# Third attention: two exponentials of each group on VectorE, and the sums two places later in TensorE's program

## What is computed

```python
xh = x.reshape(B, T, H, hd)                      # B=4, T=1024, H=16, hd=8
x_centered = xh - jnp.mean(xh, axis=1, keepdims=True)
corr = jnp.einsum('bthd,bThd->bhtT', x_centered, x_centered)
corr = jax.nn.softmax(corr, axis=-1)
out = jnp.einsum('bhtT,bThd->bthd', corr, xh)
```

## Time and profile before

| what | value |
|---|---|
| median of three runs | 3316.86 us (3312.75 to 3324.0) |
| the profiled execution, its own time | 3323.09 us |
| its span, first to last instruction | 3321.4 us |
| mean granted TensorE clock over the span | 0.941 |
| exponentials of the third attention | 496, first 2779.2 us, last 3242.6 us from the span's start |
| busy share of the span | PE 87%, ACT 72%, DVE 70%, POOL 7% |

### The profile page before, as it was taken

The page is one execution under the profiler, slowest core; times in us unless marked ns, Lnnn a source line. Parts: engine busy times, 40 slices in busy tenths (PEclk is TensorE's granted clock), DMA queues, the critical chain, the costliest instruction groups (busy, mean ns, idle before and its releaser), DMA issues. The chain is left out here.

```text
span 3321.4 us, 53185 instructions
## 1 busy us (share of the span) xinstructions
PE 2874.0 (87%) x17952; PEld 1294.0 (39%) x17952; DVE 2340.6 (70%) x3805; ACT 2377.6 (72%) x3572; POOL 224.3 (7%) x180
## 2 busy tenths in 40 slices
PE   4888888899999578888889999979979756888886
PEld 2221222666776311111147666732237551111115
DVE  6777777677776767777767777779999855443454
ACT  5889889555455679999955555556635657999994
POOL 2000000000000310000010000010000011000002
PEclk8899999999999789999989999989979967999997
DMA  5444552000000544544300000000000004233321
GB/s 130 66 61 59 68 69 42 26 0 1 0 0 1 140 81 59 66 56 65 53 32 0 0 0 0 0 28 1 1 1 0 0 22 104 40 56 47 57 49 28
DMA packets 79832, 125.47 MB, mean 38 GB/s; under 512 B 12984, under 2 KB 32344, under 8 KB 78748
## 3 DMA queue, kind: packets, MB, share of 16 engines
q1 hardware_dynamic: 79612, 122.65, 21.8%
HBM read 87.49 MB, written 29.16 MB: 35 GB/s over the span
## 5 line engine op out<-in xcount | busy, mean ns | idle before, releaser
L1952 ACT ACTIVATE m_mix_hidden<-m_mix_up_ps 128x512 f32<-128x512 f32 x512 | 305.7, 597 | 295.1 <-PE m_mix_up_ps L1868 295.1
L1129 ACT ACTIVATE b_direct_probs<-b_direct_s_ps 128x1024 f32<-128x1024 f32 x512 | 473.6, 1091 | 18.2 <-PE b_direct_o_ps L1036 11.9
L1876 PE MATMUL m_mix_down_ps<-m_w,m_mix_hidden 128*128 128x128 f32 x4096 | 474.8, 276 | 0.0
L1876 PEld LDWEIGHTS m_mix_down_ps<-m_w,m_mix_hidden 128*128 128x128 f32 x4096 | 467.2, 192 | 15.3 <-issue 15.3
L1868 PE MATMUL m_mix_up_ps<-m_mix_ZT,m_w 128*128 128x512 f32 x1024 | 471.8, 619 | 0.0
L1129 ACT ACTIVATE a_direct_probs<-a_direct_s_ps 128x1024 f32<-128x1024 f32 (+10 forms) x512 | 431.8, 938 | 54.7 <-DVE a_direct_s_ps L1167 41.9
L1129 ACT ACTIVATE c_att_probs<-c_att_s_ps 128x1024 f32<-128x1024 f32 x496 | 457.9, 1141 | 6.8 <-PE c_att_s_ps L1012 4.2
L1167 DVE SCALAR_TENSOR_TENSOR a_direct_s_ps<-distance,slopes,a_direct_s_ps 128x512 f32<-128x512 f32 (+3 forms) x512 | 355.3, 732 | 117.7 <-PE a_direct_s_ps L1012 114.7
L1164 DVE TENSOR_TENSOR b_direct_s_ps<-b_direct_s_ps,distance 128x512 f32<-128x512 f32 x512 | 335.8, 695 | 141.9 <-PE b_direct_s_ps L1012 141.0
L1036 PE MATMUL c_att_o_ps<-c_att_probs,c_v_cols 128*32 128x512 f32 x1984 | 274.9, 610 | 50.2 <-ACT c_att_probs L1129 50.2
L1036 PE MATMUL b_direct_o_ps<-b_direct_probs,v_cols 128*32 128x512 f32 x2048 | 275.1, 610 | 14.0 <-DVE b_direct_taken L1153 13.1
(11 more groups left out here) (385 smaller groups left out, 3498.5 us busy)
## 6 DMA issues: line engine op xcount, KB each, us to landing
qk_parts<-b_qkv_parts SPq DMA_DIRECT2D x48, 256.0 KB, 3.5
qk_parts<-a_qkv_parts SPq DMA_DIRECT2D x24, 256.0 KB, 4.9
a_k_rows<-qk_parts SPq DMA_DIRECT2D x32, 192.0 KB
a_q_rows<-qk_parts SPq DMA_DIRECT2D x32, 192.0 KB
b_k_rows<-qk_parts SPq DMA_DIRECT2D x32, 192.0 KB
b_q_rows<-qk_parts SPq DMA_DIRECT2D x32, 192.0 KB
qk_parts<-c_split_parts SPq DMA_DIRECT2D x24, 256.0 KB, 3.0
c_k_rows<-qk_parts SPq DMA_DIRECT2D x32, 192.0 KB
```

Of the source, the lines that this page charges most:

```text
L1129: act.activation(probs[:, J % 2, j, lo:hi], s_ps[:, slot(hg, place), lo:hi], ACT.Exp).then_inc(exped, 1)
L1876: last = pe.matmul(down_ps[:, t % 2, e, :], hidden[:, e * HALVES + h, t * P:(t + 1) * P], w["w2"][:, e * HALVES + h, :], start=(h == 0), s ...
L1952: act.activation(hidden[:, f, :], up_ps[:, f % UP_BANKS, :], ACT.Silu).then_inc(silu_done, 1)
```

## The change

Two units of each group are given instead of one: 31 at place 2 and 30 at place 6, so a group's order is 0, 1, 31, 2, 3, 4, 30, 5, ..., 29. The argument `given` becomes a list for each group, and the counts that the semaphores are compared with follow (`KEPT`, `GIVEN`, `NG`); `power` has a buffer for each given unit. VectorE's program reads the second given unit right after the two copies of the sums, ahead of the polynomial of the first. And the sums move on by as many steps as there are given units: sum J/0 to step 4J + 5, sum J/1 to step 4J + 7. The other two attentions give no units, and their programs stay as they are.

```diff
-    ORDER = [n for n in range(UNITS) if n not in given]
-    KEPT = len(ORDER)
-    NE = HG * KEPT
-    NG = len(given)
-    GIVEN_AT = (2, 15)[:NG]
-    for place, n in zip(GIVEN_AT, given):
-        ORDER.insert(place, n)
+    given = given or ((),) * HG
+    GIVEN_AT = (2, 6)
+    ORDER = [[n for n in range(UNITS) if n not in units] for units in given]
+    KEPT = [sum(len(order) for order in ORDER[:hg]) for hg in range(HG + 1)]
+    NE = KEPT[HG]
+    GIVEN = [sum(len(units) for units in given[:hg]) for hg in range(HG + 1)]
+    NG = GIVEN[HG]
+    for order, units in zip(ORDER, given):
+        for place, n in zip(GIVEN_AT, units):
+            order.insert(place, n)
...
+    def sums_at(hg, n):
+
+        return [(past, J, c) for past in (1, 0) for J in range(JT) for c in range(2)
+                if n + past * UNITS == J * GH + (GH - 1, GH + 1)[c] + len(given[(hg - past) % HG])]
...
-                        if n % GH == GH - 1:
-                            sum_up(hg, n // GH, 0, b)
-                        if n % GH == 1:
-                            if n > GH:
-                                sum_up(hg, n // GH - 1, 1, b)
-                            elif hg:
-                                sum_up(hg - 1, JT - 1, 1, b)
+                        for past, J, c in sums_at(hg, n):
+                            if hg >= past:
+                                sum_up(hg - past, J, c, b)
                             elif not first:
-                                sum_up(HG - 1, JT - 1, 1, b - 1)
+                                sum_up(HG - 1, J, c, b - 1)
                 if final:
-                    sum_up(HG - 1, JT - 1, 1, b)
+                    for n in range(GH + 2):
+                        for past, J, c in sums_at(HG, n):
+                            if past:
+                                sum_up(HG - 1, J, c, b)
...
                         take_sums(b, hg, 1)
+                        for i in range(1, len(given[after[1]]) if following else 1):
+                            take_power(*after, i)
                         if following:
                             raise_two(*after, 0)
                         if hg == 1 and not first:
                             invert(b - 1, 0)
                             invert(b - 1, 1)
-                        for i in range(1, NG if following else 1):
-                            take_power(*after, i)
+                        for i in range(1, len(given[after[1]]) if following else 1):
                             round_power(*after, i)
                             raise_two(*after, i)
...
-            for i in range(NG):
+            for i in range(len(given[0])):
                 take_power(0, 0, i)
                 round_power(0, 0, i)
                 raise_two(0, 0, i)
...
         attend_transposed(nc, f"{tag}_att", XN, operands, joined, ident, X=X, kept=const.kept_sums,
-                          given=(TPB * GH - 1,))
+                          given=((TPB * GH - 1, TPB * GH - 2),) * (HEADS // GH))
```

More of the change, by code:

```diff
@@ L848, in attend_transposed @@
         update = k.sb(f"{tag}_update", [P, 2, 4, D])
-        if given:
-            power = k.sb(f"{tag}_power", [P, SEQ])
+        if NG:
+            power = k.sb(f"{tag}_power", [P, max(len(units) for units in given), SEQ])
             whole = k.sb(f"{tag}_whole", [P, SEQ], I32)
-            raised = k.sb(f"{tag}_raised", [P, NG, SEQ])
+            raised = k.sb(f"{tag}_raised", [P, max(len(units) for units in given), SEQ])
             powers_out = k.sem(f"{tag}_powers_out")
@@ L994, in scores @@
             def scores(hg, place, b):
-                J, j = divmod(ORDER[place], GH)
+                J, j = divmod(ORDER[hg][place], GH)
                 half = hg % 2
@@ L1001, in scores @@
                 of, was = divmod(back, UNITS)
-                if ORDER[was] in given:
-                    pe.wait_ge(powers_out, b * (NG * HG) + (of * NG + given.index(ORDER[was]) + 1))
+                unit = ORDER[of][was]
+                if unit in given[of]:
+                    pe.wait_ge(powers_out, b * NG + (GIVEN[of] + given[of].index(unit) + 1))
                 else:
-                    pe.wait_ge(exped, b * NE + (of * KEPT + ORDER[was] + 1 + SLOTS))
+                    pe.wait_ge(exped, b * NE + ((KEPT[of] if of >= 0 else KEPT[HG - 1] - NE) + unit + 1 + SLOTS))
                 for c in range(2):
@@ L1021, in sum_up @@
                         pe.wait_ge(v_set, b * HG + (hg + 1))
-                    pe.wait_ge(exped, b * NE + (hg * KEPT + min(GH * (J + 1), KEPT) + SLOTS))
-                    if given and J == JT - 1:
-                        pe.wait_ge(raised_out, b * (NG * HG) + (hg + 1) * NG)
+                    pe.wait_ge(exped, b * NE + (min(KEPT[hg] + GH * (J + 1), KEPT[hg + 1]) + SLOTS))
+                    if given[hg] and J == JT - 1:
+                        pe.wait_ge(raised_out, b * NG + GIVEN[hg + 1])
                 for j in range(GH):
@@ L1034, in sum_up @@
                         n = J * GH + j
-                        weights = raised[:, given.index(n), lo:hi] if n in given else probs[:, J % 2, j, lo:hi]
+                        weights = raised[:, given[hg].index(n), lo:hi] if n in given[hg] else probs[:, J % 2, j, lo:hi]
                         last = pe.matmul(o_ps[VW * j:VW * (j + 1), c, lo - c * BANK:hi - c * BANK],
@@ L1117, in batch @@
                 for hg in range(HG):
-                    for place, n in enumerate(ORDER):
-                        if n in given:
+                    for place, n in enumerate(ORDER[hg]):
+                        if n in given[hg]:
                             continue
@@ L1173, in take_power @@
                 dve.wait_ge(scored, b * NB + (hg * UNITS + GIVEN_AT[i] + 1))
-                dve.tensor_scalar(power[:, :], s_ps[:, slot(hg, GIVEN_AT[i]), :], LOG2_E, -126.0,
+                dve.tensor_scalar(power[:, i, :], s_ps[:, slot(hg, GIVEN_AT[i]), :], LOG2_E, -126.0,
                                   ALU.mult, ALU.max).then_inc(powers_out, 1)
             def round_power(b, hg, i):
-                at = b * (NG * HG) + (hg * NG + i)
+                at = b * NG + (GIVEN[hg] + i)
                 dve.wait_ge(powers_out, at + 1)
@@ L1181, in round_power @@
                     dve.wait_ge(raised_out, at)
-                dve.tensor_copy(whole[:, :], power[:, :]).then_inc(rounded, 1)
+                dve.tensor_copy(whole[:, :], power[:, i, :]).then_inc(rounded, 1)
             def raise_two(b, hg, i):
-                at = b * (NG * HG) + (hg * NG + i)
-                done = b * (NG * HG * RAISE) + (hg * NG + i) * RAISE
-                rest, acc = power[:, :], raised[:, i, :]
+                at = b * NG + (GIVEN[hg] + i)
+                done = b * (NG * RAISE) + (GIVEN[hg] + i) * RAISE
+                rest, acc = power[:, i, :], raised[:, i, :]
                 dve.wait_ge(rounded, at + 1)
@@ L1228, in batch @@
                             invert(b, 1, 1)
-                        following = given and not (final and hg == HG - 1)
+                        following = NG and not (final and hg == HG - 1)
                         after = (b, hg + 1) if hg + 1 < HG else (b + 1, 0)
```

4 lines of the change are left out of this document (2 added, 2 removed).

## The result

The changed kernel took 3368.06 us (median of four runs, 3365.29 to 3371.99) against 3318.24 for the kernel before on the same chips: a ratio of **1.0143, 95% interval 1.0127 to 1.0158, slower by 42 to 52 us**. The forecast was slower, 3354 within 3336 to 3367; the new median is 1 us above that range, but the kernel before was slower here too, and on the forecast's own base the ratio gives 3316.86 x 1.0143 = 3364, inside it. The loss of 47 us by the ratio is larger than the forecast's 37. Between the two profiled executions the difference is 3363.6 - 3321.4 = 42.2 us of span: the changed kernel's was the fastest of its four runs, that of the kernel before lay 5 us above its median.

What follows compares the result with a forecast made beforehand. It took ScalarE's rate as the bound, TensorE close behind in order. Groups +30.8, first group +9, seams -4, last group +0.9 make +36.7 us: 3359.8 on the profiled 3323.1, 3354 against the median 3316.86; range 3336 to 3367.

Steps and rivals of the forecast that it cites:

- the chain: Ordinary groups: ScalarE waits for late sums, losing 1.87, 1.35 and 0.44 us; 30.8 us a group against 28.64, +30.8 for fourteen.
- The first group: Stage's first group: scores of place 9 wait for VectorE's late second reading, and TensorE's clock falls; +9 us, 7 to 11.
- VectorE's cover: Each group: VectorE's work of some 25.4 us fits, barely, into a round of 30.8 us.
- the last group ... with its final sums 0.2 later: Stage's last group, no group behind it: 1.35 + 0.44 lost, 0.9 saved, 0.2 old loss gone, final sums 0.2 later; +0.9 us.
- The seams: Steps between sequences and the loop's branch: of 4.9 us before, ScalarE's jump falls into its wait; -4 us.
- The branch: TensorE's loop branch, right behind sum 6/1: next scores 1.5 us later than wanted, of which 0.8 reach place 5.
- The clock: Rival, chance 5%: gaps at each group's beginning bring TensorE's clock down, each group loses 1.6 us more; 3378 us.
- A clock of 0.50 in ordinary groups: Sign in the profile after: a granted clock of 0.50 in ordinary groups would show the prediction wrong.
- ScalarE stays the bound: Rival, chance 8%: sums hide as before, every group gains 0.9 us, the first group's stall remains; 3311 us.
- Half of it: Rival, chance 7%: the second loss, at place 5, is hidden because the engines' real order is looser; +17 us, 3334.
- place 5: First exponential of block 1 in each group: waits for sum 7/1, starts at 4.97 instead of 3.62; 1.35 us lost.
- VectorE becomes the bound: Rival, chance 5%: VectorE's chain is 1.5 us longer than reckoned, groups last 31.5 instead of 30.8 us; 3364 us.

Runs made afterwards that it cites:

- e1: The changed kernel with the sums one place later instead of two: 3341.64 us, ratio 1.0052 to the kernel before.
- e3: The changed kernel with one given unit, as in the kernel before, and the sums one place later: 3337.14 us, ratio 1.0046 to the kernel before.
- e4: The changed kernel with room for three blocks of exponentials instead of two: 3336.49 us, ratio 1.0041 to the kernel before.
- e7: The changed kernel with three blocks of room, sums one place later, second given unit at place 8, both read first in the first group: 3320.08 us, ratio 0.9989.
- e2: The changed kernel with both given units read before the first polynomial in the first group: 3363.83 us, ratio 1.0117 to the kernel before.
- e5: The changed kernel with the second given unit's polynomial left out, so its output is incomplete: 3363.74 us, ratio 1.0123 to the kernel before.
- e6: The changed kernel with TensorE adding zeros four times in its gap where a group ends: 3364.57 us, ratio 1.0124 to the kernel before.

## Why the prediction was right, and where it was short

**The place, the mechanism and the size of a group: right.** The waits of 1.51 and 1.21 us stand where the chain put them, after the same sums, and a group lasts 30.82 us against the 30.8 worked out. The chains of the same pieces gave 28.9, 29.5, 28.4 to 28.6 and 27.7 to 27.9 for e1, e3, e4 and e7, and 28.93, 29.51, 28.37 and 27.73 were measured. e4 shows the cause by taking the room's shortage away, e3 by adding the delay alone.

**The first group: right.** +9 forecast, 39.21 - 30.19 = +9.0 measured; e2 takes 8.3 of it back. TensorE worked at 1.2 GHz again behind the stall, as forecast: its granted clock was 0.51 in the mean until 2795.8. (The parts listed for the group at full clock add up to 37.3, not 37.4 us.)

**VectorE's cover: right within groups, wrong at the stage's end.** It fits, with 2.04 us to spare, and e5 shows that its work costs a group nothing. But "the last group ... with its final sums 0.2 later" left out what else is queued on VectorE there, the two reciprocals behind the second polynomial, and "the transfers and GpSimd's copies ... are not waited for" does not hold for the last inverses. From the last exponential to the LoRA layer it is 19.15 us against 16.00, so +3.2 in place of +0.2: the last sums start 0.6 us later, and from there to TensorE's product with the inverses it takes 9.4 us instead of 7.6, since it waits for GpSimd; the last 0.7 us lie behind that. e5 has 15.88. What the prediction could not price from its rows is the long instruction at 3271.46: VectorE had no idle time between it and the reciprocals, so 2.0 of the 3.2 us may be its doing. That is an estimate; no run takes it away alone.

**The seams: mis-sized.** "-4" was -2.8. ScalarE's own jump does not fall into its wait: the three steps over seams took 31.54, 31.44 and 31.44 us, 0.6 or 0.7 more than the others, as before. The branch, priced at 0.8, took 0.21 us in this execution and cost nothing; the group behind it took 32.42 us, 1.6 more than others, for a fall of the clock.

**The clock: a rival that came in part.** It was put as all or nothing at 1.6 us a group. It came in four of the fourteen ordinary groups (32.1 to 32.4 us) and in the last, which in e2 and e6, without a fall there, is 1.5 us shorter: together +7.2. A clock of 0.50 in ordinary groups was one of the prediction's own signs of being wrong; for these groups it was. The reason against it, "the gaps before that size never brought it down", counted each gap for itself, where each beginning now has two close together, 1.15 and 0.53 us, with a short run of scores between; that it takes the pair is not shown, only that filling the first ended the falls (e6). That such gaps would do nothing to the clock did not hold: it fell behind 5 of 15.

By the trace the sum is: the fourteen ordinary groups 33.3 (30.5 for the chain, 5.6 for the clock, -2.8 for the seams), the first group +9.0, the last +2.2 (1.5 of it the clock), the stage's end +3.2, together 47.7 us, close to the ratio's 47. The forecast's 36.7 is 11 us short of it: 7.2 for the clock, 3.0 for the stage's end, 1.2 for the seams, -0.4 for the chain and the last group. The stretch ahead of the stage was 3.2 and the LoRA layer 2.3 us shorter than in the kernel before, which the change didn't touch; so the spans differ by 42.2 only. How many falls a run meets and how long its branch takes differs; the runs without a trace can't show it. (The terms of the forecast's own range, added up, give 3344 to 3367 instead of 3341 to 3365.)

So it was in part luck that the time fell inside the range: two terms that were put at nothing or at 0.2, the clock and the stage's end, took 10 of the 11 us above the forecast.

**The rivals.** "ScalarE stays the bound": no, e1 and e4. "Half of it": no, place 5 costs its 1.21. "VectorE becomes the bound": no, e5; in e7 it is late at the stage's end.

## What to carry to other kernels

Where one engine fills a buffer and another empties it, count for each wait how many instructions the filling engine has left while the wait's chain runs, at the seams of the groups above all: work taken off it there shortens that lead as well. Moving work to an engine that has room also moves what is queued behind it: look at the first group, where no earlier group covers, and at the last, where nothing follows. The bound was ScalarE with 99.8% of its time busy, and yet relieving it of 3% cost 1.4%. A third block took an ordinary group from 30.8 to 28.4 us, and only with the sums nearer and the first group mended (e7) did the stage get shorter than before.

## What the runs showed of the hardware

TensorE's clock fell from 2.4 to 1.2 GHz though TensorE stood idle for no more than 1.15 us at a time: it had been busy 1.80 of the 3.40 us before. It fell behind 5 of 15 such places; which ones, the traces don't tell.

VectorE's instructions on 128 x 1024 elements in SBUF, 0.69 or 1.23 us long, took some 2 us more when they met GpSimd's product of `c_joined` and the inverses (2.4 to 3.4 us long). That shows in every trace, one to four times in the stage (28 times in the eleven), and nowhere else in it. The reciprocals at the stage's end, on PSUM, kept their 3.36 us beside it.

The loop's branch on TensorE's sequencer took 3.3 to 5.0 us in ten traces and 0.21 in the eleventh, the change's. What makes it short or long is not shown.

The LoRA layer behind the stage does the same work in every kernel here, but lasted 59.3, 61.6 and 63.6 us in the change, the kernel before and e7, at a mean granted clock of 0.76, 0.71 and 0.66:

```profile
3304.30:3363.60 59.30, 38.16 (x256) 35.13 (x256) 28.54 (x67) 25.80 (x88) 9.81 (x5) 0.76 0.14 39
```

```profile
3259.80:3321.40 61.60, 40.79 (x256) 36.59 (x256) 28.67 (x67) 25.81 (x88) 9.81 (x5) 0.71 0.13 38
```

```profile
3254.90:3318.50 63.60, 42.90 (x256) 38.96 (x256) 28.69 (x67) 25.91 (x88) 9.80 (x5) 0.66 0.13 37
```

So 4 us between two kernels may come from a later layer that neither changes, by how long TensorE's clock is low there; what decides that no run shows. A gain of that size is to be read from the stage itself.
